# Expert weights loaded where their low halves will stand, every input tile kept on chip, and the heads of batch 0 laid out while the experts run

## The reference

```python
xn = layernorm(x)                                   # no scale, no bias
# attention: 8 heads of 8 features
qk = (xn @ Wqk.T + bqk).reshape(b, n, 8, 8, 2)      # q is [..., 0], k is [..., 1]
v  = (xn @ Wv.T + bv).reshape(b, n, 8, 8)
attn = softmax(q @ k.T) / 8                         # per batch and head, 512 x 512
a  = (attn @ v).reshape(b, n, 64) @ Wo.T + bo
# experts: the 2 best of 8 for every token
top = top_k(xn @ W_gate + b_gate, 2)
y  = relu(einsum('bsd,edh->bseh', xn, W_e) + b_e)   # only the 2 chosen ones are needed
out = x + a + mean(y of the 2 chosen experts)
```

## Time and profile before

| | |
|---|---|
| median of three runs | 362.17 us (360.97 to 363.67) |
| profiled execution, its own time | 359.6 us |
| its span | 357.9 us |
| stage one ends (last projection) | 56.5 us |
| first expert matmul | 85.0 us |
| last expert matmul ends | 223.5 us |
| PE busy | 312.8 us, 87% of the span |
| POOL, DVE, ACT busy | 210.1, 238.3, 170.6 us |
| DMA | 59.59 MB, 167 GB/s on the mean |

### The profile page before, as it was taken

One profiled execution on the slowest core, in us unless ns is written; L12 is line 12 of the kernel. 1 busy time (PEld: TensorE's weight loads), 2 busy tenths in 40 slices (PEclk: granted clock), 3 DMA queues, 4 the chain that ended last, 5 costly groups with the idle time before them and its releaser, 6 DMA issues.

```text
span 357.9 us, 5578 instructions
## 1 busy us (share of the span) xinstructions
PE 312.8 (87%) x1629; PEld 223.1 (62%) x1629; DVE 238.3 (67%) x557; ACT 170.6 (48%) x295; POOL 210.1 (59%) x227
## 2 busy tenths in 40 slices
PE   2786793587999999999999989589999999999964
PEld 1586793475888888888888767245556555553412
DVE  3878868861444344757678895998787978883313
ACT  1878881111333333333233224457777667586740
POOL 3386999746567676775656722885688887000000
PEclk9999887555999999999999999789999999999996
DMA  7999992405354555654344411469998999410113
GB/s 225 313 404 395 321 275 93 208 5 172 98 167 159 165 176 158 196 187 157 131 152 145 117 59 60 120 173 182 317 234 159 229 178 141 114 39 0 60 59 117
DMA packets 31003, 59.59 MB, mean 167 GB/s; under 512 B 5504, under 2 KB 5632, under 8 KB 30848
## 3 DMA queue, kind: packets, MB, share of 16 engines
q1 hardware_dynamic: 20864, 39.59, 31.4%
q0 software_dynamic: 7728, 18.62, 24.8%
q10 hardware_dynamic: 2384, 1.04, 1.1%
HBM read 38.52 MB, written 18.61 MB: 160 GB/s over the span
## 4 chain that ended last, share of the span: by engine, by line
PE 78%; DVE 11%; issue 4%; ACT 4%; DMA 2%; POOL 0%; SPq 0%; DVEq 0%; POOLq 0%; ACTq 0%
PE ps_s L1118 31%; PE ps_t L1050 10%; PE ps_o L1065 8%; PE ps_s L979 7%; PE ps_s L1039 7%; PE ps_t L1098 5%; PE ps_t L965 2%; PE ps_m L1010 2%; DVE hot_row L819 1%; DMA row_in<-in_L_attn_x_dram 1%; ACT probs L654 1%; PE ps_m L1022 1%; PE ps_m L1014 1%; DVE v_ones L890 1%; PE ps_o L1039 1%
## 5 line engine op out<-in xcount | busy, mean ns | idle before, releaser
L1118 PE MATMUL ps_s<-w_split,t_hi 128*128 x312 | 101.7, 407 | 2.2 <-issue 1.9
L654 ACT ACTIVATE probs<-ps_t 128x512 f32<-128x512 f32 x128 | 69.7, 596 | 31.7 <-PE ps_t L1050 30.1
L845 DVE TENSOR_REDUCE row_max<-ps_s 128x1 f32<-128x512 f32 x112 | 72.0, 683 | 12.5 <-PE ps_s L1039 12.0
L493 POOL TENSOR_TENSOR row_mid<-row_mid,bias_o 128x512 f32<-128x512 f32 x39 | 50.6, 1297 | 47.4 <-ACT row_mid L599 47.4
L599 ACT ACTIVATE row_mid<-row_mid 128x512 f32<-128x512 f32 x39 | 24.7, 632 | 94.7 <-DVE row_mid L866 94.7
L1118 PEld LDWEIGHTS ps_s<-w_split,t_hi 128*128 128x128 f32 x312 | 56.7, 192 | 13.7 <-issue 3.3
L1118 PE MATMUL ps_s<-w_split,t_lo 128*128 x156 | 61.9, 397 | 0.0
L1050 PE MATMUL ps_t<-q_t,k_head 128*128 128x512 f32 x128 | 57.0, 457 | 3.1 <-ACT probs L654 2.7
L519 POOL DMA_INDIRECT acc<-expert_rows,slots_i x32 | 49.7, 1552 | 14.5 <-issue 8.7
L1050 PEld LDWEIGHTS ps_t<-q_t,k_head 128*128 128x128 f32 x128 | 23.9, 191 | 43.7 <-ACT probs L654 31.4
L866 DVE TENSOR_TENSOR row_mid<-ps_s,bias_e 128x512 f32<-128x512 f32 x39 | 27.0, 692 | 32.1 <-PE ps_s L1118 30.9
(11 more groups left out here) (134 smaller groups left out, 431.1 us busy)
## 6 DMA issues: line engine op xcount, KB each, us to landing
expert_rows<-row_mid SPq DMA_DIRECT2D x39, 256.0 KB, 2.0
stage<-in_L_ffn_W_e_dram SPq DMA_DIRECT2D x16, 512.0 KB, 7.9
xn_rows<-row_mid SPq DMA_DIRECT2D x16, 256.0 KB, 6.2
acc<-in_L_attn_x_dram SPq DMA_DIRECT2D x16, 256.0 KB, 7.1
out_dram<-res SPq DMA_DIRECT2D x16, 256.0 KB, 2.0
row_in<-in_L_attn_x_dram SPq DMA_DIRECT2D x8, 256.0 KB, 6.2
w_split<-in_L_attn_x_dram SPq DMA_DIRECT2D x8, 256.0 KB, 8.6
bias_e<-in_L_ffn_b_e_dram SPq DMA_DIRECT2D x1, 2048.0 KB, 7.5
```

The costliest lines, as they stand in the source:

```text
L493: pool.tensor_tensor(row_mid[:, n % 4, :], row_mid[:, n % 4, :], bias_o[:], ALU.add).then_inc(y_done, 1)
L654: act.activation(probs[:, n % 2, j, :], ps_t[:, j % 2, :], ACT.Exp).then_inc(exp_done, 1)
L845: dve.tensor_reduce(row_max[:, b % 2, h, i:i + 1], score_bank(n), AX.X, ALU.max).then_inc(max_done, 1)
L1118: mm = pe.matmul(ps_s[:, n % 2, :], a[:, n % 2, ks], rhs, start=(k == 0), stop=(k == 3 * KC - 1))
```

## The change

Stage one: the halves of the expert weights are no longer loaded into `stage` but straight into the place of their own low part. ACT reads them there, and POOL overwrites them with the low part. So no load waits for a place. The first six halves (`WF`) are issued by ACT before its first computation, half i+6 by SP once tile i is normalised. All 16 tiles of `x` have places of their own; SP issues eight at once (`XF`) and tile i+8 once tile i is normalised. The loads of `Wo` and of the output bias move from ACT's queue to SP's, behind the first normalised tile. ACT makes the high part of half i in round i, where it was half i-1.

Routing: some pairs of small DVE instructions become one. `hot_val` is made by ACT (16 activations with the token number as scale) and not by DVE (8). The list of experts of the tiles is computed behind `gather_i`, no longer ahead of it, and POOL's fourth gather waits for it, since its target stands on the same bytes. The layout of the heads of batch 0 moves from here into the expert stage: k behind tile 1 and q behind tile 7 on POOL, turned by PE behind tiles 6 and 10.

`lay_out` handles four token tiles with four instructions, where it had sixteen. For batch 1 it is done at once behind one expert tile, and PE turns these heads behind tiles 34 and 35.

```diff
-RW = 5
-RX = 14
+XF = 8
+WF = 6
+K0_AT, Q0_AT = 6, 10
-K_AT, Q_AT = LAY_AT + QT - 1, LAY_AT + QT
+K_AT, Q_AT = LAY_AT + 1, LAY_AT + 2
...
+        def w_half(c, part):
+            e, half = divmod(c, 2)
+            return w_split[:, e, part, 2 * half:2 * half + 2, :]
+        def load_w(queue, c):
+            e, half = divmod(c, 2)
+            src = we[e].rearrange("(c p) h -> p c h", p=P)[:, 2 * half:2 * half + 2, :]
+            queue.dma_start(w_half(c, 1).bitcast(F32), src).then_inc(w_in[c], 16)
...
-            for i in tiles:
-                for at in hi_at:
-                    eng.tensor_copy(heads[:, i, :, at:at + HE].bitcast(F32R), exact[:, i]).then_inc(step, 1)
-                eng.memset(heads[:, i, :, 0:2], first).then_inc(step, 1)
-                steps[0] += 3
+            for at in hi_at:
+                eng.tensor_copy(heads[:, :, :, at:at + HE].bitcast(F32R), exact).then_inc(step, 1)
+            eng.memset(heads[:, :, :, 0:2], first).then_inc(step, 1)
+            steps[0] += 3
             eng.wait_ge(step, steps[0])
-            for i in tiles:
-                eng.tensor_tensor(heads[:, i, :, lo_at:lo_at + HE], exact[:, i], heads[:, i, :, hi_at[0]:hi_at[0] + HE],
-                                  ALU.subtract).then_inc(laid, 1)
+            eng.tensor_tensor(heads[:, :, :, lo_at:lo_at + HE], exact, heads[:, :, :, hi_at[0]:hi_at[0] + HE],
+                              ALU.subtract).then_inc(laid, 1)
...
 # SP, in the loop over the 16 tiles, behind the write of the normalised tile i
-                if i + RI + 2 < NT:
-                    load_x(i + RI + 2)
-                if i + 2 < NT:
-                    load_w(i + 2)
+                if i == 0:
+                    sp.dma_start(wo_dst[:, :, 0:HD], wo_src).then_inc(wo_in, 16)
+                    sp.dma_start(wo_dst[:, :, HD:2 * HD], wo_src).then_inc(wo_in, 16)
+                    sp.dma_start(bias_o[:], bo.rearrange("(a d) -> a d", a=1).to_broadcast([P, D])).then_inc(bias_o_in, 16)
+                if i + XF < NT:
+                    load_x(i + XF)
+                if i + WF < 2 * NE:
+                    load_w(sp, i + WF)
...
 # ACT
-            act.dma_start(wo_dst[:, :, 0:HD], wo_src).then_inc(wo_in, 16)
-            act.dma_start(wo_dst[:, :, HD:2 * HD], wo_src).then_inc(wo_in, 16)
-            act.dma_start(bias_o[:], row(bo)).then_inc(bias_o_in, 16)
+            for c in range(WF):
+                load_w(act, c)
...
+            tiles = hot_tile[:].rearrange("p (r i) n -> p r i n", r=2)
+            for i in range(NT):
+                g, k = divmod(i, 2)
+                if g >= 3:
+                    act.wait_ge(hot_used, g - 2)
+                act.activation(hot_val[:, g % 3].rearrange("p (r k) n -> p r k n", r=2)[:, :, k, :], tiles[:, :, i, :],
+                               ACT.Copy, scale=token_f[:, i:i + 1]).then_inc(values_hot, 1)
...
 # DVE, behind hot_row
+            dve.wait_ge(tokens_found, 1)
+            dve.tensor_copy(gather_i[:], ps_s[:, 1, 0:NS]).then_inc(gather_ready, 1)
             link(dve.tensor_tensor(ecol[:, 3, :], ecol[:, 1, :], ecol[:, 2, :], ALU.add))
...
-                    if 0 <= n - LAY_AT < QT:
+                    if n == LAY_AT:
                         dve.wait_ge(lay_zero, 2)
                         for which in ("k", "q"):
-                            lay_out(dve, dve_step, steps, 1, which, (n - LAY_AT,))
+                            lay_out(dve, dve_step, steps, 1, which)
```

More of the change, by code:

```diff
@@ L97, in attention_and_experts @@
         rout = ExitStack()
-        top_f = sb("top_f", [P, NT, 8], F32, rout)
+        hot_tile = sb("hot_tile", [P, NC, NSE], F32, rout)
+        slot_p = sb("slot_p", [P, 2, NT, NE], F32, rout)
+        top_f = sb("top_f", [P, 2, NT], F32, rout)
         pick = sb("pick", [P, 2, NT, NE], F32, rout)
@@ L180, in attention_and_experts @@
         weights_split = sem("weights_split")
-        x_in = [sem(f"x_in{s}") for s in range(RX)]
+        x_in = [sem(f"x_in{i}") for i in range(NT)]
         xn_out = [sem(f"xn_out{s}") for s in range(4)]
@@ L191, in attention_and_experts @@
         proj_kept = sem("proj_kept")
-        w_in = [sem(f"w_in{s}") for s in range(RW)]
+        w_in = [sem(f"w_in{c}") for c in range(2 * NE)]
         w_hi_made = sem("w_hi_made")
@@ L228, in attention_and_experts @@
         acc_in = [sem(f"acc_in{i}") for i in range(NT)]
-        ya_in = [sem(f"ya_in{i}") for i in range(NT)]
-        yb_in = [sem(f"yb_in{i}") for i in range(NT)]
+        y_in = [sem(f"y_in{i}") for i in range(NT)]
         y_relu = sem("y_relu")
@@ L307, in norm_group, with lay_out @@
             return [first <= i < end for first, end in GROUPS].index(True)
-        def lay_out(eng, step, steps, b, which, tiles=range(QT)):
+        def lay_out(eng, step, steps, b, which):
             s, first, hi_at, lo_at, laid = ((0, 0.0, (2, 10), 18, q_laid[b]) if which == "q" else
@@ L551, in split_w @@
             def split_w(c):
-                e, half = divmod(c, 2)
-                act.wait_ge(w_in[c % RW], 16 * (c // RW + 1))
-                act.activation(w_split[:, e, 0, 2 * half:2 * half + 2, :], stage[:, c % RW, :, :],
-                               ACT.Copy).then_inc(w_hi_made, 1)
+                act.wait_ge(w_in[c], 16)
+                act.activation(w_half(c, 0), w_half(c, 1).bitcast(F32), ACT.Copy).then_inc(w_hi_made, 1)
             def hi(i):
@@ L626, in _ @@
             KEPT = ("k", "q", "max", "turn")
-            for job in FIRST:
-                keep(*job)
             for n in range(NS + 1):
@@ L797, in _ @@
             link(dve.tensor_tensor(place[:, 0:NT, :], ps_c[:, 0:NT, :], ecol[:, 0:1, :].to_broadcast([P, NT, NE]), ALU.add))
-            for r in range(2):
-                dve.tensor_tensor(slot_p[:, r], place[:, 0:NT, :], pick[:, r], ALU.mult).then_inc(dve_step, 1)
-            steps[0] += 2
-            dve.wait_ge(dve_step, steps[0])
+            link(dve.tensor_tensor(slot_p[:], place[:, 0:NT, :].unsqueeze(1).to_broadcast([P, 2, NT, NE]), pick[:], ALU.mult))
             link(dve.tensor_reduce(slot_f[:], slot_p[:], AX.X, ALU.add))
@@ L1077, in _ @@
             mm.then_inc(counted, 1)
-            for job in FIRST[:2]:
-                fill(*job)
             for c in range(NC):
                 if c % 4 == 0:
-                    pe.wait_ge(hot_ready, 2 * (c // 4 + 1))
+                    pe.wait_ge(hot_ready, c // 4 + 1)
+                    pe.wait_ge(values_hot, 2 * (c // 4 + 1))
                 at = (c // 4) % 3, c % 4
@@ L1088, in _ @@
             mm.then_inc(tokens_found, 1)
-            for job in FIRST[2:]:
-                fill(*job)
             def turn_rows(n):
```

121 lines of the change are left out of this document (47 added, 74 removed).

## The result

The changed kernel takes 364.45 us, the median of 20 runs (362.11 to 367.17); the kernel before, run beside it, 362.3 us (20 runs, 359.78 to 364.69). The profiled execution took 363.67 us and spans 361.9 us, 4.0 us more than the 357.9 us of the profile before. Both kernels spread over some 5 us from run to run.

What follows compares the result with a forecast made beforehand. PE was taken to bound the expert stage, DVE the routing's hot loop, and DMA and POOL stage one. The terms 1.5 - 1.35 + 1.85 + 1.5 - 1.9 = +1.6 us on 362.17 gave 363.8 us, range 358.3 to 367.5.

Steps and rivals of the forecast that it cites:

- Stage one, +1.5: Loads and low parts before routing: more weight halves ahead delay x tiles and POOL's end by 1.5 us.
- The hole of 9 to 12 us: Stage one: DMA engines not full then; six early halves were to fill it, winning back 1.7 us.
- the third rival: Stage one: ACT's early issues stall and shift its first activation by 2 to 4 us; 366.8 us, chance 0.16.
- the prediction's own last paragraph: Forecast wrong if POOL's run starts by 30.4, ACT's first activation passes 10.5 us, or PE's hot-loop clock is up.
- the step's own sum: Stage one, tile 11: four more halves cost 5.2 us, less 1.8 us to spare and 1.7 for the DMA hole.
- free second queues: Stage one: a rule by which loads on another engine's queue delay nothing, making the term 0; the prediction rejected it.
- Routing, -1.35: Routing: merged instructions and no `hot_val` on DVE; PE's 32 matmuls set the end, `gather_i` 1.35 us sooner.
- Heads of batch 0, +1.85: Expert stage: two fills of eight transposes moved onto PE there cost 1.85 us.
- Heads of batch 1 at once, +1.5: Expert stage, tile 34: one idle stretch of PE and a slower clock cost 4.15 us against 2.6 before, +1.5.
- a fall from stage one: PE's clock at 0.51 after 1.90 us idle; expected again at tile 34, losing 1.7 us.
- Start of attention, -1.9: DVE's layout of batch 2: eight larger instructions in 2.4 us for 32 in 4.3, saving 1.9 us.
- POOL lays out at the same time: Start of attention: the gain's lower bound, -0.8 us, if POOL's simultaneous layout makes instructions grow.

Runs made afterwards that it cites:

- e7: The kernel of e2 with four idle activations ahead of ACT's first work, so that ACT starts late; 364.53 us.
- e1: The changed kernel with its six early weight halves issued by SP behind x tiles 0 to 7 instead of by ACT; 364.02 us.
- e5: The changed kernel with the heads of batch 0 laid out and turned in the routing again, merged layouts kept; 363.29 us.
- c235: The changed kernel with the edits of e2, e3 and e5 together; 353.4 us.
- c23: The changed kernel with the edits of e2 and e3 together; 354.77 us.
- e4: The kernel before with only the merged head layouts, that of batch 1 made in one go; 359.9 us.
- e3: The changed kernel with POOL's six memsets of head tiles moved behind DVE's layout of batch 2 and POOL's of batch 3; 359.08 us.
- e6: The kernel before with POOL's six memsets moved behind DVE's layout of batch 2, as in e3; 356.02 us.
- e2: The changed kernel with weight halves issued by SP at the old pace, two ahead and one per tile, and split one tile later; 361.62 us.
- e8: The changed kernel with twelve tiles of x issued at the start instead of eight; 367.01 us.
- e9: The kernel of c235 with POOL's last low part held back until DVE has made mask; 353.5 us.

## Why the prediction was right, and where it was not

The direction (no change within 1%), the range and nearly the value (363.8 against 364.45) came true. The steps did not, and their errors offset each other.

- **Stage one, +1.5: measured +4.5.** Two things failed. The hole of 9 to 12 us, from which the prediction took back 1.7 us, is not filled by early halves: the share stayed at 0.51. And ACT does start late: the third rival, given 0.16, was the larger part of the matter (3.5 us of delay by tile 7, ahead of any wait for the tiles from 8 on). Its condition (issues that end after 8 us, a first activation past 10.5) was met, with issues up to 11.6, a first activation at 12.93 and a shift of 3.5 us of the 2 to 4 it named; by the prediction's own last paragraph the forecast was wrong then. e7 prices the late start at 3.0 us alone; in the changed kernel the early halves add 1.1 us to it (34.83 against 33.76), which two single profiles hardly resolve. Without the credit for the hole the step's own sum is 5.2 - 1.8 = 3.4 us, and e1 shows 3.2, but with SP's stall in it, so this agreement is in part luck. The mechanism for the order is the one given in kind: behind four more halves tile 8 lands 2.6 us later after its issue (9.5 against 6.9 us in e7) and tile 11 1.4 us later (9.7 against 8.3), not 5.2. Tile 11 was issued at 23.80 instead of 17.91, for SP issues it only behind the store of the fourth row tile, which waits for ACT; with ACT late and two halves ahead (e7) it was issued at 22.34.

The prediction set the Trainium skill ("DMA: Bandwidth & Descriptors", "Issuing engines are not separate DMA queues") against free second queues. The landing times of tile 8 side with the page on the transfers: halves on ACT's queue made a tile on SP's queue land later. It adds that issuing on several engines only saves the sequencer's time, "usually small relative to the DMA itself"; here 7.61 us of issuing on ACT, with 3.5 us of them past the point where it was wanted, were not small.

- **Routing, -1.35: measured -1.38** from `mask` to `gather_i`, for the reasons given: PE at half clock sets the end, 7.0 us for 32 matmuls.

- **Heads of batch 0, +1.85: measured +1.75** by the two rows, 1.7 by the profiles set side by side in e5. The net price in the time was smaller, 1.2 us (e5) and 1.4 (c235 against c23), because in the routing the move takes POOL's copies out of DVE's way, for which nothing had been forecast.

- **Heads of batch 1 at once, +1.5: measured -0.8 to -1.0** (e4). This step had the wrong sign, and two parts of it were wrong. The idle stretch was 1.73 us, not 2.2. And the clock did not fall behind it: I carried over a fall from stage one, where PE had already been working with gaps, to a stage where PE had run without one. That this difference is the reason is not shown.

- **Start of attention, -1.9: measured +1.5 between the two profiles.** The instructions got as short as forecast (1.95 us for the layout), and that was worth 0.76 us where nothing blocks (e3 against e6). But the profile of before held 2.96 us for 16 numbers and 3.84 us for four copies, which I passed over; the bound "POOL lays out at the same time" looked at the wrong instructions of POOL. In the changed kernel the block took another form, 6.53 us in front of PE's first values instead of 2.96. e3 and e6 show that it was there in both kernels, 5 to 6 us of time in each, and e4, which has none of the new loads, shows the 6.53 us too. I had no rival for it. The +1.5 may belong to that one execution of the kernel before: by the medians the memsets cost the kernel before 6.0 us and the changed one 5.4, and with the 0.76 us the step is -1.4 us, an estimate; e4 gives about the same (2.2 us in all, less the 0.8 to 1.0 of batch 1). The intervals of these medians are over 1 us wide, so the size stays open.

In short, between the two profiles and against the forecast: +3.0 in stage one, -2.5 on batch 1, +3.4 at the start of attention, and -1.5 in small parts (routing and batch 0 -0.25 together, the first expert tile -0.6, the tail -0.6). That makes 4.0 us where 1.6 were forecast, of which 1.9 are the choice of the two executions; the medians stand 2.15 us apart. A forecast within 0.7 us owed more to errors that offset each other than to its steps.

## What to carry to other kernels

Look for short instructions with long durations on DVE and POOL before costing an edit beside them: what stood behind 16 numbers in 2.96 us was worth more (6 us in the kernel before) than any step of the change. Two causes that delay the same event do not add, and taking one away shows little while the other stands; try both alone and together, and look whether the edit that takes one away puts a new wait in its place, as in e1. One profile is one execution: compare a stage over the profiles of several kernels that do the same work in it. Loads issued early by a computing engine cost that engine the time of issuing once many are outstanding, and push back what stands behind them in the order.

## What the hardware showed unexpectedly

- **A blocked DVE instruction stays blocked over several of POOL's.** Beside POOL's addition and six memsets, which followed each other without a gap, the TENSOR_SCALAR took 6.53 us in seven of these kernels' profiles (the changed one, e1, e2, e4, e5, e7, e8), each time up to POOL's last memset; in the profile of before 2.96; with the memsets away 1.18, up to the end of the addition. The Trainium skill ("SBUF — State Buffer", "Who interferes with whom") says that DVE (in a mode that uses both port pairs, which `copy`, `cast` and `tensor_scalar` can enter) and GpSimd share a pair of SBUF ports as an exclusive lock: whoever issues first has it for the whole instruction, and the other fully blocks. The runs agree that it blocks fully; they add that the wait was not over with the one instruction but lasted over several, and that in one profile of eight the instruction got in between two memsets. That it is this lock is the page's account; the runs show only whose instruction ends the wait.
- **The same at the end of stage one.** `pick` took 2.50 us beside POOL's subtraction of 2.35 us and 0.43 us without it (e9); the page names that pair, two inputs in SBUF against an instruction of POOL that reads it.
- **Issuing slows when much is outstanding.** Six issues of 512 KB took 7.61 us on ACT and 7.37 us on SP, one of `bias_o` 4.29 us (e1); halves issued one per tile took 0.43 to 0.61 us each (e2). That the number outstanding is the cause is read from this alone.
- **1.73 us of idle PE left the clock at 1.00** behind more than 100 us in which PE had been busy throughout (110 of 110 us from 90 to 200), while 1.90 us in stage one were followed by 0.51, and 4.82 us at the start of attention by 0.50.
